# A trees layer whose looked-up rows get a fifth place, and whose second rows are worked ahead of the next sequence's first rows

## The reference

```python
logits = x @ W_in.T + b_in
act = jax.nn.gelu(logits, approximate=False)
act4 = act.reshape(B, P, G, FAN)
decisions = jnp.argmax(act4, axis=-1)
for d in range(DEPTH):
    moves = jnp.take_along_axis(decisions, current[..., None], axis=2)[..., 0]
    next_platform = platform + FAN ** d
    current = next_platform + FAN * (current - platform) + moves
    nodes.append(current)
...
masked = act4 * mask[..., None]
new_logits = masked.reshape(B, HID) @ W_out.T
```

## Time and profile before

| | us |
|---|---|
| median of three runs | 2145.59 |
| lowest and highest | 2142.69, 2166.28 |
| the profiled execution | 2149.68 |
| its span, first to last instruction | 2147.9 |
| busy in the span: PE, DVE, ACT, POOL | 1648.2, 1221.2, 850.6, 464.6 |
| the trees layer in the span | 586 to 969 |
| look-ups (L2321): 128, busy and idle before | 132.7 and 324.8 |

### The profile page before, as it was taken

The page is one execution under the profiler, slowest core; times in us unless marked ns, Lnnn a source line. Parts: engine busy times, 40 slices in busy tenths (PEclk is TensorE's granted clock), DMA queues, the critical chain, the costliest instruction groups (busy, mean ns, idle before and its releaser), DMA issues. The chain is left out here.

```text
span 2147.9 us, 34926 instructions
## 1 busy us (share of the span) xinstructions
PE 1648.2 (77%) x12368; PEld 1139.4 (53%) x12368; DVE 1221.2 (57%) x4315; ACT 850.6 (40%) x1792; POOL 464.6 (22%) x611
## 2 busy tenths in 40 slices
PE   3368646798878867745589979996886777999888
PEld 1147433454537656644345447763554654677666
DVE  5965645564277768642376623335766876766332
ACT  1142335355327556552245543332553420333423
POOL 0001000220022433420243100003201214655211
PEclk8655777799879988977699989986997866999979
DMA  2000001220034564640322000002211000000000
GB/s 80 0 11 1 9 29 46 71 57 19 7 112 164 207 227 158 225 169 6 102 75 76 22 16 0 0 27 64 54 33 58 1 1 1 2 2 2 2 1 21
DMA packets 79748, 115.69 MB, mean 54 GB/s; under 512 B 8416, under 2 KB 60512, under 8 KB 78816
## 3 DMA queue, kind: packets, MB, share of 16 engines
q0 software_dynamic: 18432, 67.38, 9.0%
q1 hardware_dynamic: 58560, 45.00, 7.5%
q10 hardware_dynamic: 2592, 1.18, 0.2%
HBM read 88.95 MB, written 1.05 MB: 42 GB/s over the span
## 5 line engine op out<-in xcount | busy, mean ns | idle before, releaser
L2321 POOL DMA_INDIRECT f_rows<-tree_table,f_index x128 | 132.7, 1037 | 324.8 <-DVE f_index L2377 153.4
L2534 PE MATMUL f_ps_o<-f_rows,shared_sb 128*128 128x128 f32 x1024 | 136.1, 299 | 71.0 <-ACT f_rows L2606 71.0
L2534 PEld LDWEIGHTS f_ps_o<-f_rows,shared_sb 128*128 128x128 f32 x1024 | 131.7, 212 | 76.7 <-ACT f_rows L2606 73.8
L1469 ACT ACTIVATE x_probs<-x_ps_z 128x768 f32<-128x768 f32 (+1 forms) x128 | 117.5, 918 | 104.6 <-PE x_ps_z L1334 66.4
L2606 ACT ACTIVATE f_rows<-f_rows,f_low_act 128x128 f32<-128x128 f32 x512 | 152.9, 387 | 0.8
L2416 DVE CUSTOM_DVE_ANT_0 f_rows<-f_rows,f_xn 128x128 f32<-128x128 f32 x512 | 111.4, 287 | 59.9 <-DMA f_rows<-tree_table,f_index 59.9
L1173 DVE TENSOR_REDUCE x_minus_max<-x_ps_s 128x4 f32<-128x1024 f32 x64 | 78.2, 1224 | 63.0 <-PE x_ps_s L1334 62.7
L3052 ACT ACTIVATE r_probs<-r_ps_z 128x768 f32<-128x768 f32 x64 | 51.9, 811 | 67.5 <-PE r_ps_z L2943 67.5
L1794 PE MATMUL f_ps_h<-f_xnT,weights 128*128 128x512 f32 x144 | 76.8, 661 | 2.3 <-ACT f_hT L1859 2.3
L1806 PEld LDWEIGHTS f_ps_y<-weights,f_hT 128*128 128x128 f32 x576 | 70.3, 193 | 14.3 <-issue 12.6
L1859 ACT ACTIVATE f_hT<-f_ps_h,weights 128x512 f32<-128x512 f32 x72 | 48.6, 685 | 69.8 <-PE f_ps_h L1794 68.1
(11 more groups left out here) (651 smaller groups left out, 4196.2 us busy)
## 6 DMA issues: line engine op xcount, KB each, us to landing
x_queries<-x_pieces SPq DMA_DIRECT2D x96, 64.0 KB, 2.1
x_keys<-x_pieces SPq DMA_DIRECT2D x84, 64.0 KB, 2.1
a_queries<-a_pieces SPq DMA_DIRECT2D x48, 64.0 KB, 2.1
weights<-w_L_ffn SPq DMA_DIRECT2D x1, 2985.5 KB, 10.1
a_keys<-a_pieces SPq DMA_DIRECT2D x42, 64.0 KB, 2.1
weights<-w_L_ffn SPq DMA_DIRECT2D x1, 2449.0 KB, 11.0
weights<-w_L_ffn SPq DMA_DIRECT2D x1, 2176.0 KB, 8.5
f_rows<-tree_table,f_index POOLq DMA_INDIRECT x128, 6.0
```

Of the source, the lines that this page charges most:

```text
L1469: a.activation(probs[:, r % HELD, :, :], ps_z[:, :, 0:WIDE], ACT.Exp, scale=scale).then_inc(exped, 1)
L2321: pool.indirect_dma_start(rows[:, u % 2, j, tree, :], None, g.tree_table, bass.IndirectOffsetOnAxis(index[:, u % 2, low, j * TREES + tree: ...
L2534: last = pe.matmul(ps_o[:, low, j, :], g.ident, rows[:, u % 2, j, tree, OUT + f * D:OUT + (f + 1) * D], start=k == 0, stop=k == TREES * FA ...
```

## The change

The rows get five places instead of four, used in a ring by half units: half `j` of sequence `u` has place (2u + j) mod 5. So a half of the next sequence's first rows can be looked up before the last half's second rows are summed. POOL asks in step h for the first rows of h+1 ahead of the second rows of h. On DVE, ACT and PE a step now works the second rows of h-1 ahead of the first rows of h, and the two ways down come one right after the other, followed by the dense descent. `low_act` gets a third buffer, and a fifth semaphore counts the landings. To make room, the split of the bias works in the fifth place and in the bias's own memory, for which one more copy is made.

```diff
+    PLACES = 5
-        low_act = sb("low_act", [P, 2, Q, FAN])
+        low_act = sb("low_act", [P, 3, Q, FAN])
-        rows = sb("rows", [P, 2, HALVES, TREES, ROW])
+        rows = sb("rows", [P, PLACES, TREES, ROW])
...
-            for low, u in ((0, h), (1, h - 1)):
+            for low, u in ((1, h - 1), (0, h)):
...
+        place = lambda u, j: (u * HALVES + j) % PLACES
+        gathered_in = lambda u, j: gathered[place(u, j)]
...
+            def gather(low, u, j):
+                pool.wait_ge(index_ready, pointed[low, u, j if low else 0] + 1)
+                pool.sem_inc(may_gather, 1)
+                last_user = divmod(u * HALVES + j - PLACES, HALVES)
+                before = (0, u, j) if low else (1, *last_user)
+                if before in order_at:
+                    pool.wait_ge(summed, order_at[before] + 1)
...
+            for h in range(UNITS):
                 for j in range(HALVES):
...
+                    if h + 1 < UNITS:
+                        gather(0, h + 1, j)
+                for j in range(HALVES):
+                    gather(1, h, j)
...
-                step(v.tensor_copy(bias_rows[:, :], whole))
+                step(v.tensor_copy(bias_left[:, :], whole))
+                step(v.tensor_copy(bias_rows[:, :], bias_left[:, :]))
...
+                if before:
+                    dots(1, h - 1, 0)
+                if h >= 2:
+                    finish(h - 2)
+                if before:
+                    dots(1, h - 1, 1)
+                    add_low(0, h - 1)
                 if here_now:
                     dots(0, h, 0)
...
                     dots(0, h, 1)
...
                     go_down(h, 0)
...
                     go_down(h, 1)
...
-                if here_now:
-                    sum_low(0, h, 0)
+                if before:
+                    sum_low(1, h - 1, 0)
                 if next_too:
                     sum_dense(h + 1, 1)
                 if ahead:
                     project(h + 3, 0)
+                if before:
+                    sum_low(1, h - 1, 1)
+                if here_now:
+                    sum_low(0, h, 0)
+                if ahead:
+                    project(h + 3, 1)
                 if here_now:
                     sum_low(0, h, 1)
...
+                if before:
+                    gelu_low(1, h - 1, 0)
+                    scale_rows(1, h - 1, 0)
                 if next_too:
                     take_masked(h + 1, 1)
                 if ahead:
                     take_xT(h + 3)
+                if before:
+                    gelu_low(1, h - 1, 1)
+                if here_now:
+                    gelu_low(0, h, 0)
+                if before:
+                    scale_rows(1, h - 1, 1)
+                if here_now:
+                    gelu_low(0, h, 1)
+                    scale_rows(0, h, 0)
+                if ahead:
+                    activate(h + 3, 0)
                 if here_now:
                     scale_rows(0, h, 1)
```

More of the change, by code:

```diff
@@ L2273, in layer1_trees @@
         maskedT = sb("maskedT", [P, ALL, P])
-        bias_rows, ones_rows = sb("bias_rows", [3, sum(WIDTHS)], BF16), sb("ones_rows", [3, P], BF16)
-        bias_left, bias_part, kept = sb("bias_left", [3, sum(WIDTHS)]), sb("bias_part", [3, sum(WIDTHS)]), sb("kept", [3, 3])
-        rows = sb("rows", [P, 2, HALVES, TREES, ROW])
+        ones_rows, kept = sb("ones_rows", [3, P], BF16), sb("kept", [3, 3])
+        rows = sb("rows", [P, PLACES, TREES, ROW])
+        bias_left, bias_part = (rows[0:3, PLACES - 1, :, :].rearrange("p t r -> p (t r)")[:, i * sum(WIDTHS):(i + 1) * sum(WIDTHS)]
+                                for i in range(2))
+        bias_rows = w["bias"][0:3, 0:sum(WIDTHS) // 2].bitcast(BF16)
         ps_t, ps_in, ps_d, ps_o = ps("ps_t", [P, 512]), ps("ps_in", [P, 3, 512]), ps("ps_d", [P, 4, D]), ps("ps_o", [P, LOW, 4, D])
@@ new lines, in gather @@
+            def gather(low, u, j):
[5 more added lines that the diff above has]
+                    pool.wait_ge(summed, order_at[before] + 1)
+                    pool.sem_inc(may_gather, 1)
+                for tree in range(TREES):
+                    pool.indirect_dma_start(
+                        rows[:, place(u, j), tree, :], None, g.tree_table,
+                        bass.IndirectOffsetOnAxis(index[:, u % 2, low, j * TREES + tree:j * TREES + tree + 1], 0),
+                    ).then_inc(gathered_in(u, j), 16)
@@ L2410, in dots @@
             def dots(low, u, j):
-                v.wait_ge(gathered_in(u, j), (u // 2 * LOW + low + 1) * TREES * 16)
-                sums = low_act[:, u % 2, trees_of(j), :]
+                v.wait_ge(gathered_in(u, j), ((u * HALVES + j) // PLACES * LOW + low + 1) * TREES * 16)
+                sums = low_act[:, u % 3, trees_of(j), :]
                 for k in range(TREES * FAN):
                     tree, f = divmod(k, FAN)
-                    row = rows[:, u % 2, j, tree, f * D:(f + 1) * D]
+                    row = rows[:, place(u, j), tree, f * D:(f + 1) * D]
                     last = v.tensor_tensor_reduce(row, row, xn[:, u % KEPT, j, :], 1.0, 0.0,
-                                                  ALU.mult, ALU.add, low_act[:, u % 2, j * TREES + tree, f:f + 1])
+                                                  ALU.mult, ALU.add, low_act[:, u % 3, j * TREES + tree, f:f + 1])
                 step(last)
-                v.tensor_tensor(sums, sums, rows[:, u % 2, j, :, 2 * OUT:ROW], ALU.add).then_inc(dots_ready, 1)
+                v.tensor_tensor(sums, sums, rows[:, place(u, j), :, 2 * OUT:ROW], ALU.add).then_inc(dots_ready, 1)
             def go_down(u, j):
@@ L2423, in go_down @@
                 v.wait_ge(low_ready, order_at[0, u, j] + 1)
-                step(descend(low_act[:, u % 2, q, :], u, q))
+                step(descend(low_act[:, u % 3, q, :], u, q))
                 point(1, u, q)
@@ L2533, in sum_low @@
                     tree, f = divmod(k, FAN)
-                    last = pe.matmul(ps_o[:, low, j, :], g.ident, rows[:, u % 2, j, tree, OUT + f * D:OUT + (f + 1) * D],
+                    last = pe.matmul(ps_o[:, low, j, :], g.ident, rows[:, place(u, j), tree, OUT + f * D:OUT + (f + 1) * D],
                                      start=k == 0, stop=k == TREES * FAN - 1)
@@ L2596, in gelu_low @@
             def gelu_low(low, u, j):
-                part = low_act[:, u % 2, trees_of(j), :]
+                part = low_act[:, u % 3, trees_of(j), :]
                 a.wait_ge(dots_ready, order_at[low, u, j] + 1)
@@ L2604, in scale_rows @@
                     tree, f = divmod(k, FAN)
-                    row = rows[:, u % 2, j, tree, OUT + f * D:OUT + (f + 1) * D]
-                    last = a.activation(row, row, ACT.Copy, scale=low_act[:, u % 2, j * TREES + tree, f:f + 1])
+                    row = rows[:, place(u, j), tree, OUT + f * D:OUT + (f + 1) * D]
+                    last = a.activation(row, row, ACT.Copy, scale=low_act[:, u % 3, j * TREES + tree, f:f + 1])
                 last.then_inc(scaled, 1)
@@ L3518, in build @@
         g.x_loaded = ctx.enter_context(nc.semaphore("x_loaded"))
-        g.gathered = [ctx.enter_context(nc.semaphore(f"gathered{j}")) for j in range(TILES)]
+        g.gathered = [ctx.enter_context(nc.semaphore(f"gathered{j}")) for j in range(TILES + 1)]
         first_stats = ctx.enter_context(nc.semaphore("first_stats"))
```

52 lines of the change are left out of this document (3 added, 49 removed).

## The result

The changed kernel takes 2170.10 us as the median of 20 runs (2161.18 to 2181.34), the kernel before 2153.37 (2137.29 to 2166.28) beside it: a ratio of 1.0078, with a 95% interval of 1.0057 to 1.0099. The forecast was 2142, a small gain; it came out as a small loss. The forecast had started from the 2145.59 us of the first three runs. Counted as changes, 3.9 us less were forecast and 16.7 more were measured, 20.6 apart.

The account below looks back on a forecast made before the run. Bound: POOL's look-ups wait for a free place, DVE for the look-ups. 685.4 + 4 x 39.3 + 3 x 36.5 + 13 = 965.1 against 969.02, 3.9 us earlier, so 2142 from a median of 2145.59; range 2129 to 2160.

Parts of the forecast that it names:

- The walk through a turn: One step followed over DVE, ACT, PE, POOL from S to the next S: 39.3 us, 36.5 without a projection.
- Half 0's look-up is held by the mask multiplication: POOL's second-row look-up at S+22.2, possibly held by DVE: turn 40.7 if held, 38.0 if free, 39.3 taken.
- The tail from the last S: From the last S to the stage's last addition: 12.4 us, or 15 at PE's lower clock; 13 taken.
- S: The moment DVE starts the second rows of half 1, from which a turn is counted; the first forecast at 685.4.
- step 4: POOL's four look-ups of second rows' half 1: 8.9 us from first issue to landing, so landed at S+38.0.
- The sum: The stage's forecast end: 685.4 + 4 x 39.3 + 3 x 36.5 + 13 = 965.1, against 969.02 before.
- POOL is free by S+14, ahead of 22.2: POOL's new wait costs nothing: it is free by S+14, before half 0's second rows are asked for at S+22.2.
- The first issue of half 1: POOL's first look-up of second rows' half 1: S+30.4 with a projection, S+27.6 without.
- Start: The first step gets longer on ACT and PE: first S at 685.4, where the old second step began at 671.94.
- The slower rival: Second rows hold the loop longer at PE, one more sum at low clock: turn 43.4, 2175 us; 16 in 100.
- break-even turn of 39.9: The turn with a projection above which the change loses; above 42.9 it loses over 1%.
- The faster rival: Look-ups land in 6.5 us, not 8.9, so DVE's 33 to 36 us bounds: 2120 us; 7 in 100.

Follow-up runs that it names:

- e10: Changed kernel without any look-ups of first rows from the fourth sequence on: 2162.14 us, ratio 1.0036 to the kernel before.
- e8: The changed kernel itself once more, nothing altered, for a second profile: 2172.70 us.
- e4_start: Changed kernel with ACT's and PE's order of the kernel before in the first step alone: 2160.72 us, ratio 1.0031 to the kernel before.
- e7: Changed kernel with the edits of e1 and e4_start together: 2170.27 us, ratio 1.0076 to the kernel before.
- e3_ring_old: Changed kernel with the old DVE, PE, ACT order; POOL asks next first rows' half 0, second rows, then half 1: 2129.38 us, ratio 0.9885.
- e2: Changed kernel whose first rows' look-ups move 128 of 1028 numbers from the fourth sequence on: 2172.26 us, ratio 1.0084 to the kernel before.
- e9_hold_dots: Changed kernel; POOL asks for next first rows only after dot products of second rows and this sequence's first rows: 2179.27 us, ratio 1.0101.
- e1: The hold: changed kernel, POOL asks for next first rows only after the second rows' dot products: 2172.62 us, ratio 1.0089 to the kernel before.
- e6: e1 with second rows of half 0 moving 128 of 1028 numbers from the second sequence on: 2175.83 us, ratio 1.0102 to the kernel before.

## Why the prediction was wrong

- **What it took over rightly.** The walk through a turn held. DVE waits for DMA at second rows only. The first rows are always there. The wait for PE stays POOL's largest in total. Half 0's look-up is held by the mask multiplication in some steps, 2.82, 3.03 and 3.04 us long at 670.40, 839.16 and 881.22. The tail from the last S was 13.1 (forecast 13).
- **The step that failed first: step 4, "That is 8.9 from first issue to landing".** It is about 10.2 us (e10, seven cases of 9.6 to 10.8, and 10.2 for the very group of the kernel before that the step reads). The 8.9 was read off a DMA share of 0.05, which was not yet zero. The sum holds it eight times, in the first S and in seven turns: 8 x 1.3 = 10.4 us of the 26.8. That is an account by terms: in the five steps with a stall S follows DVE's own late work, so a faster landing alone would not have won all of it.
- **The step that was missing: what the look-ups do to other engines.** The prediction asked of the moved look-ups only whether POOL is free in time ("POOL is free by S+14, ahead of 22.2") and whether DVE holds POOL. It never priced look-ups stopping DVE. The trace of before gave no sign of it: dot products lie there beside four look-ups after a pause, and take 3.7 us, but hardly ever beside the second or third group of a row. In the changed kernel S comes later than the landing by 6.9 us in seven turns (78.3 from first issue to S, less 7 x 10.2) and by some 2 in the first step: 8.8 us.
- **The first issue of half 1.** It was forecast at S+30.4 with a projection and S+27.6 without, 204.4 us in seven turns, and took 209.8; in the first step it came 2.1 late. Together that is 7.5 us. Without the first rows' look-ups it takes 201.8 (e10). Most of it is the stall again, passed on by ACT and PE: where half 0's dot products stop, its rows are scaled later, and PE's first sum of the step starts 4.0 to 5.2 us after S (first three turns, after a stall) instead of 2.25 (fourth, after none; 1.8 to 3.9 were forecast). From that sum on PE works without a pause to the one that POOL waits for. In the three turns without a projection half 1's look-ups stand right behind half 0's on POOL. PE's timeline in the first turn (S 689.36) and at the start of the fourth (S 816.93):

```profile
694.56 6.21 PE L2537 MATMUL f_ps_o<-f_rows,shared_sb 128*128 128x128 f32 x32 [6.07 <-ACT f_rows L2609]
...
717.21 3.84 PE L2537 MATMUL f_ps_o<-f_rows,shared_sb 128*128 128x128 f32 x32
...
819.18 5.37 PE L2537 MATMUL f_ps_o<-f_rows,shared_sb 128*128 128x128 f32 x32 [5.56 <-ACT f_rows L2609]
```

- **Sum of the miss:** 10.4 + 8.8 + 7.5 + 0.1 (tail) = 26.8. The second profile of the changed kernel (e8) misses by 22.4 in the same terms: 10.4 + 8.4 + 3.9 - 0.3. The first two terms hold in both, the third varies with the steps that stall. In e10, whose later steps have no stall, the seven turns miss the forecast by 6.2: 8.8 for the landing, and 2.6 less than forecast up to the first issue. Where nothing stalls, then, the walk up to the first issue holds to 2.6 us.
- **Start.** The sum gave the first S 99.2 us from the stage's start; it took 104.5, from the same three causes. e4_start shows that the choice of the new order for ACT and PE in the first step costs 9 to 10 us in the changed kernel, more than half of the whole loss by the runs. It is not a term of its own: beside the hold (e7) no such gain is seen.
- **The rivals.** The slower rival named the right sign and nearly the time (2175), but not the mechanism: it wanted one more of PE's sums at the lower clock in each turn. In the turns with a projection only the first sum of a step is slow, as it was before (6.21 us at 694.56, behind 6.07 us of idle, with a granted clock of 0.59; 5.4 to 6.5 us in the other three turns); the later three sums take 3.7 to 3.8 each at a granted clock of 1.00. Its break-even turn of 39.9 did its work: the turns with a projection took 42.5, and the loss follows. The faster rival was tested by e10: with first rows gone the landing did not fall to 6.5.
- **Why not more.** The change made the second rows late instead of the first ones: they are asked for and used with nothing between but a transfer of 10 us. e3_ring_old shows that the fifth place, with POOL's asking fitted to it, was worth about 24 us in the old order; the new order gave that back, and 17 more.

**Open.** What in the issuing of look-ups stops the other engines was not found. The first rows' bytes are not it (e2), and a long row of look-ups alone does not do it either: the kernel before issues twelve in a row from 783.06 to 799.74, beside a sum on PE (788.71 to 792.55) and a descent on DVE, and nothing stops. Of the six stalls in the profile of the changed kernel, only one has an instruction fetch on the DMA queues between its first gap and its end (at 687.31). That the hold gains in the stage of its profiles and nothing in the runs is not explained either, beyond that single executions of one kernel differ by 10 us and more. Nor was it found why some steps stall and others of the same layout do not.

## What to carry to other kernels

A transfer has landed when the receiver can start, not when the DMA share falls: read the landing from first issue to the start of an instruction that waited for it, or from the trace's own time to landing, since the tail at a share of 0.05 was worth 1.3 us here, eight times over. Before moving DMA issues next to other engines' work, look whether the trace has a place where as many of them lie side by side with that work as the change will put there. Four look-ups after a pause cost the dot products nothing here, the second or third group of a row up to 3.9 us; where no such place exists, the cost is unknown and belongs into the range. And where a change has two parts, a buffer and an order, forecast and run each alone: the buffer, with a fitting order of asking, won 1.1% here, while with the new order of the other engines the kernel lost 0.8%.

## What was not expected of the hardware

- DVE's dot products beside a run of look-ups: 3.7 us became 6.2 to 7.6 in two profiles of the changed kernel, in gaps of 0.2 to 1.1 us between instructions and often a last one of 2.1 to 2.8, though the profile names no data that DVE waited for; with the bytes cut to an eighth it was 4.8 to 7.3.
- The same gaps on PE when the look-ups were moved beside its sums: 0.46, 1.76 and 0.47 us in one sum. The Trainium skill (SBUF — State Buffer, Who interferes with whom) knows a lock between VectorE and GpSimd, and says that TensorE and ScalarE never wait on anyone; in e9_hold_dots TensorE stood all the same, so that lock alone is not what these gaps are.
- Four look-ups of 0.5 MB in one group took 9.2 to 10.8 us from first issue to the released engine, whether the group ahead of them moved all its bytes or an eighth (e1, e6), and with or without another group behind (10.0 at 816.93 with one, 9.6 to 10.8 in e10 without).
